# Softmax attention in two passes: the first pass runs three units ahead of its consumer instead of two, TensorE's block work moves in front of its second-pass pieces, and VectorE's splits are spread one per step

## What is computed

```
def adaptive_temperature_softmax(logits):
    original_probs = softmax(logits)
    entropy = sum(-original_probs * log(original_probs + 1e-09))
    poly_result = POLY[0]*e2*e2 + POLY[1]*e2*entropy + POLY[2]*e2 + POLY[3]*entropy + POLY[4]
    beta = where(entropy > 0.5, maximum(poly_result, 1.0), 1.0)
    return softmax(logits * beta)
sim = einsum('bhid,bhjd->bhij', q, k) / sqrt(hd), masked above the diagonal
out = einsum('bhij,bhjd->bhid', adaptive_temperature_softmax(sim), v) @ Wo.T + bo
```

## Time and profile before

| | |
|---|---|
| median of three runs | 2244.86 us |
| the profiled execution, its own time | 2242.96 us |
| its span in the trace | 2241.2 us |
| busy in the span | PE 1608.5, DVE 1480.7, ACT 1393.1, POOL 141.7 us |
| attention, from the first exp1 to the end of its last window | 755.4 to 1960 us |
| ACT busy in the attention's windows | 1051.0 of 1204.6 us |

### The profile page before, as it was taken

How to read it: one execution, slowest core, us unless ns; L and a number is a source line. 1 busy time by engine, 2 the same in 40 slices (tenths; PEclk the granted TensorE clock), 3 DMA queues, 4 the chain that set the end, 5 groups by cost and what they waited for, 6 DMA issues and landing times. The chain is left out here.

```text
span 2241.2 us, 22322 instructions
## 1 busy us (share of the span) xinstructions
PE 1608.5 (72%) x6402; PEld 689.7 (31%) x6402; DVE 1480.7 (66%) x3478; ACT 1393.1 (62%) x2635; POOL 141.7 (6%) x126
## 2 busy tenths in 40 slices
PE   4787899999999643777767778667777787511166
PEld 2443344444444201222222222223222233201144
DVE  6645354535464798887787787877878774479922
ACT  3564443434333697899987999879999997300012
POOL 0000000000000100000000000000000000035365
PEclk9898899999999755676666765666666769755578
DMA  4000065454556201101011010010110103240031
GB/s 146 0 0 0 13 162 156 131 154 132 155 150 171 58 32 39 62 33 62 24 39 60 33 50 34 31 71 26 42 40 28 54 13 98 58 122 0 0 102 49
DMA packets 56667, 147.36 MB, mean 66 GB/s; under 512 B 7760, under 2 KB 22480, under 8 KB 53936
## 3 DMA queue, kind: packets, MB, share of 16 engines
q1 hardware_dynamic: 52320, 136.63, 20.6%
q0 software_dynamic: 3072, 8.39, 1.2%
q10 hardware_dynamic: 1152, 0.92, 0.3%
HBM read 126.38 MB, written 19.53 MB: 65 GB/s over the span
## 5 line engine op out<-in xcount | busy, mean ns | idle before, releaser
L1682 DVE CUSTOM_DVE_ANT_0 sa_lg<-sa_e,sa_lg 128x1024 f32<-128x1024 f32 (+7 forms) x512 | 386.4, 755 | 93.4 <-ACT sa_lg L1573 92.9
L1423 PE MATMUL sa_ps<-sa_space 72*128 72x512 bf16 (+3 forms) x768 | 293.0, 450 | 212.5 <-DVE sa_nmax L1673 148.0
L1563 ACT ACTIVATE sa_e<-sa_e,sa_nmax 128x1024 f32<-128x1024 f32 (+7 forms) x512 | 415.9, 812 | 36.2 <-DVE sa_nmax L1673 36.1
L1673 DVE CUSTOM_DVE_ANT_0 sa_e<-sa_ps,sa_mask 128x1024 f32<-128x1024 f32 (+7 forms) x512 | 385.5, 753 | 71.3 <-PE sa_ps L1423 69.9
L1573 ACT ACTIVATE sa_lg<-sa_e,sa_sum 128x1024 f32<-128x1024 f32 (+7 forms) x512 | 414.9, 810 | 5.1 <-DVE sa_prod L1682 4.6
L1581 ACT ACTIVATE sa_p<-sa_ps 128x512 f32<-128x512 f32 x576 | 345.8, 626 | 40.8 <-PE sa_ps L1475 30.9
L1472 PE MATMUL sa_ps<-sa_q2s,sa_k2s 75*128 75x512 bf16 (+3 forms) x768 | 298.0, 432 | 66.9 <-ACT sa_p L1581 55.2
L974 DVE TENSOR_TENSOR mx_hw<-mx_spread,mx_h 128x512 f32<-128x512 f32 x256 | 176.0, 691 | 232.8 <-PE mx_ps L813 193.3
L875 ACT ACTIVATE mx_h<-mx_ps 128x512 f32<-128x512 f32 (+1 forms) x264 | 157.0, 597 | 277.0 <-PE mx_ps L800 256.4
L800 PE MATMUL mx_ps<-mx_f,m 128*128 128x512 f32 x512 | 262.0, 597 | 0.8 <-ACT mx_h L875 0.8
L813 PE MATMUL mx_ps<-mx_hw,m 128*128 128x512 f32 x512 | 259.9, 594 | 0.6 <-DVE mx_hw L974 0.6
(11 more groups left out here) (322 smaller groups left out, 1864.3 us busy)
## 6 DMA issues: line engine op xcount, KB each, us to landing
mx_spread<-mx_spill SPq DMA_DIRECT2D x256, 256.0 KB, 4.0
sa_space<-sa_spill_q SPq DMA_DIRECT2D x96, 96.0 KB
sa_space<-sa_spill_k SPq DMA_DIRECT2D x96, 96.0 KB
sa_k2s<-sa_spill_k SPq DMA_DIRECT2D x48, 192.0 KB
sa_q2s<-sa_spill_q SPq DMA_DIRECT2D x48, 192.0 KB
m<-m_in SPq DMA_DIRECT2D x1, 4256.0 KB, 18.7
records<-sa_e SPq DMA_DIRECT2D x8, 512.0 KB, 5.2
be_w<-w_in SPq DMA_DIRECT2D x16, 256.0 KB, 12.5
```

The source lines that it names most:

```text
L1423: last = nc.tensor.matmul(out[:, col:col + w], q_ring[:, c % 2, local, i * P:(i + 1) * P], k_ring[:, c % 2, local, col:col + w], start=Tru ...
L1563: nc.scalar.activation(e[:, u % 5, 0:w], e[:, u % 5, 0:w], ACT.Exp, scale=-1.0, bias=nmax[:, b % 2, i, h:h + 1], accum_out=sums[:, b % 2, ...
L1673: nc.vector.tensor_tensor_reduce(out=e[:, u % 5, 0:w], in0=slot_of("unit", u)[:, 0:w], in1=mask_wide[:, SEQ - w:SEQ], scale=1.0, scalar=3. ...
L1682: nc.vector.tensor_tensor_reduce(out=lg[:, u % 2, 0:w], in0=e[:, u % 5, 0:w], in1=lg[:, u % 2, 0:w], scale=1.0, scalar=0.0, op0=ALU.mult, ...
```

## The change

- `AHEAD` goes from 2 to 3: score and evacuate of unit u + 3 are issued at step u. The prologue does three units instead of two.
- On TensorE the loop over `pieces2_at(u + 1)` moves from behind the score to the end of the step, behind all blocks.
- The block steps move so that TensorE still finds the unit ahead in the other slot: `WIDE_AT` 7 to 8, `SHIFT_AT` 9 to 10, `A_AT` 83 to 84, `Q_AT` 87 to 86, `K_AT` 89 to 94, `V_AT` 107 to 108, and `TURN_AT`, `ATT_AT`, `PROJ_AT` each one later.
- VectorE's chains are dealt out: `temper` at step 3, `set_beta` at 4, `split_shift` at 5; the splits of the widened queries at 9, 10, 11 (two) and 12; those of the projected queries at 87, 88, 90, 91 and 92; those of the keys at 95, 97 and 99.
- Three second-pass banks, five `e` buffers, two `lg` buffers and every instruction's shape stay. The number of instructions stays. SyncE's program is the same row by row.

```diff
-AHEAD = 2
+AHEAD = 3
...
-        WIDE_AT, SHIFT_AT = 7, 9
-        A_AT, Q_AT, K_AT, V_AT = 83, 87, 89, 107
-        TURN_AT, ATT_AT, PROJ_AT = 9, 13, 17
+        WIDE_AT, SHIFT_AT = 8, 10
+        A_AT, Q_AT, K_AT, V_AT = 84, 86, 94, 108
+        TURN_AT, ATT_AT, PROJ_AT = 10, 14, 18
...
-            yield from (("unit", 0), ("unit", 1))
+            yield from (("unit", u) for u in range(AHEAD))
...
                     if u + AHEAD < ALL1:
                         score(u + AHEAD)
-                    for m in pieces2_at(u + 1):
-                        second(m)
-                        if m % GROUP == GROUP - 1 and m >= GROUP:
-                            answer(m // GROUP - 1)
                     if (k := side_at(u, WIDE_AT)) is not None:
                         widen(k)
...
                     if (b := scores_at(u, 18)) is not None:
                         score_experts(b)
+                    for m in pieces2_at(u + 1):
+                        second(m)
+                        if m % GROUP == GROUP - 1 and m >= GROUP:
+                            answer(m // GROUP - 1)
...
                     if (k := side_at(u, 2)) is not None:
                         entropy(k)
+                    if (k := side_at(u, 3)) is not None:
                         temper()
-                    if (k := side_at(u, 3)) is not None:
+                    if (k := side_at(u, 4)) is not None:
                         set_beta(k)
-                    if (k := side_at(u, 4)) is not None:
+                    if (k := side_at(u, 5)) is not None:
                         split_shift(k)
...
-                    for r in (8, 9, 10):
-                        if (k := side_at(u, r)) is not None:
-                            split_q2(k, range(2 * (r - 8), min(5, 2 * (r - 8) + 2)))
+                    for r, steps in ((1, range(0, 1)), (2, range(1, 2)), (3, range(2, 4)), (4, range(4, 5))):
+                        if (k := side_at(u, WIDE_AT + r)) is not None:
+                            split_q2(k, steps)
...
                     if (b := batch_at(u, Q_AT)) is not None:
                         take_q(b)
-                        split_q(b, range(0, 3))
-                    if (b := batch_at(u, Q_AT + 1)) is not None:
-                        split_q(b, range(3, 5))
+                    for r, step in ((1, 0), (2, 1), (4, 2), (5, 3), (6, 4)):
+                        if (b := batch_at(u, Q_AT + r)) is not None:
+                            split_q(b, (step,))
                     if (b := batch_at(u, K_AT)) is not None:
                         take_k(b)
-                    if (b := batch_at(u, K_AT + 1)) is not None:
-                        split_k(range(2, 4))
-                    if (b := batch_at(u, K_AT + 2)) is not None:
-                        split_k(range(4, 5))
+                    for r, step in ((1, 2), (3, 3), (5, 4)):
+                        if (b := batch_at(u, K_AT + r)) is not None:
+                            split_k((step,))
```

8 lines of the change are left out of this document (4 added, 4 removed).

## The result

The changed kernel takes 2260.02 us (median of 12 runs) against 2245.07 us for the kernel before (12 runs, same chip): 1.0062 times as long, with a 95% interval of 1.0052 to 1.0072. It is 0.6% **slower** where the prediction said about 0.9% faster. The profiled execution took 2260.62 us with a span of 2258.7 us, against 2241.2 before.

A forecast was written before the change was run, and what follows sets the result against it. It took ACT as the attention's full engine, idle only around blocks, where DVE is nearly the bound. 6.0 + 0.8 + 13.0 + 0 = 19.8 us off 2242.96 gave 2223.2; plus 1.9 for the median, 2225 us, range 2206 to 2246.

The forecast's parts named there:

- A new wait: Away from blocks on DVE, evacuate(u + 3) directly behind the product it waits for: 0.12 us each, bounds 0 and 0.23.
- 154 waits: New waits in stretches where DVE is the bound: about 154, 18.5 us, of which 4.0 fall into idle time.
- First stretch, side 0 and first projections: DVE becomes the bound and is 3.4 us late at side 0; better spread then pays for the wait: 0.
- Sides' ends: Shift earlier, fewer evacuation waits: 1.5 us less in four windows (6.0), 0.4 in two with layernorm behind (0.8).
- Projections: Two windows like 1160 to 1244: splits no longer bunched, 84 us becomes 77.5, 6.5 us less each, 13.0 in all.
- Tail: Steps beyond the first pass's units: DVE runs free, the chain over HBM starts from the same splits: 0.
- Those of the order: Projection windows' ACT idle 18.5 to about 12 us, evacuation waits well below 36, `take_shift` about 2 to 3 instead of 3.7.
- Those of the wait: First stretch: product to evacuation 0.12 us more, first exp1 to that of unit 64 about 3 us more.
- Rival 2: Slower: new wait and late products, in the first stretch and windows after blocks, eat everything; 2251 us, chance 0.12.
- turning point of 0.25 us: Size of the new wait at which the gain of 20 us over about 154 waits turns into a loss.
- Rival 1: DVE is not the bound and the wait is free, all blocks hidden: about 2200 to 2210 us, chance 0.2.
- Rival 3: Order swap and later steps cancel, waits only change their names: 2 to 4 us less, 2242 us, chance 0.1.

The follow-up runs named there:

- E2: The kernel before with four of its five e buffers used, so evacuate(u + 2) waits for its direct predecessor product(u - 2): 2253.92 us, 1.0096 of the kernel before.
- E1: The changed kernel with six e buffers instead of five, so evacuate(u + 3) waits for product(u - 3): 2224.94 us, 0.9974 of the kernel before.
- E3: The changed kernel with five e buffers and, from step 512 on, pieces in front of the blocks again: 2242.75 us, 1.0049 of the kernel before.
- E4: The changed kernel with six e buffers and, from step 512 on, pieces in front of the blocks again: 2221.45 us, 0.9958 of the kernel before.
- E12: The kernel before with only TensorE's pieces moved behind the blocks, still two units ahead: 2229.04 us, 0.9995 of the kernel before.
- E15: The kernel before with AHEAD 3, blocks one step later, six e and three lg buffers, pieces in front, chains bunched: 2213.18 us, 0.9933 of the kernel before.
- E5: The changed kernel with six e buffers, three lg buffers and pieces in front from step 512 on: 2230.39 us, 0.9934 of the kernel before.
- E7: The kernel before with AHEAD 3, blocks one step later, six e and two lg buffers, pieces in front, chains bunched: 2237.2 us, 0.9959 of the kernel before.

## Why the prediction was wrong

**The step that failed** is "A new wait": "I take 0.12 us", between bounds of 0 and 0.23. It measured 0.22, and 0.23 in E2. The reasoning was that "the 0.11 of the plain pair covers a tail of that size", the accumulator read's 0.08. It doesn't: 0.08 and 0.11 add up, and 0.03 more. (The bound of 0.23 was to be these two in full, but they make 0.19; the measured wait lies above their sum.) The Trainium skill, "VectorE: DVE Perf Modes", section "The DRAIN you can't avoid", would have 0 for a semaphore between chained instructions; the 0.11 us of the earlier trace rows and the 0.22 here are against it. The linked pair comes 62 times in the first stretch, where DVE had 4.0 us of idle time. E1 against the changed kernel puts the wait at 0.9% of the time, about 20 us; the traces have 10.3 of it in the first stretch and 18.8 by exp1(511). (For the same pair E3 and E4 the traces have 27.1 by exp1(511), so what lies outside the first stretch is known to some 8 us only.)

The wait decides the sign, as E1 shows, but the prediction's own sum would not have said so. With 0.22 in place of 0.12 its 154 waits cost 15.4 us more, which makes 2240, still a little faster than 2245. The rest is what the prediction put at nothing: the piece behind `widen` at the sides, and the tail.

*First stretch, side 0 and first projections: predicted 0 (3.4 late, won back).* It came out at +12.0, 11.1 late and nothing won back. With 0.22 the prediction's own formula gives 62 x 0.22 - 4.0 = 9.6 for the first part. Without the wait (E1, E4) 0.8 of the 11.1 remain, and the whole is at +0.5.

*Sides' ends: predicted 6.0 + 0.8 us less.* They came out at 4.7 more. In the three sides' windows together ACT's idle time went from 36.3 to 40.2 us. Waits for evacuations fell from 9.4 to 0 and `take_shift` from 21.5 to 12.2, but waits for pieces (L1472) rose from 0 to 14.0, for products from 0.5 to 6.1 and for layernorm's subtraction (L96) from 4.6 to 7.5. Over the whole attention `take_shift` fell by 29.0 - 17.6 = 11.4 over eight, more than the 1.0 each that was taken. What the prediction left out is that the piece behind `widen` waits for the block (2.35 us on ACT in the timeline). That alone doesn't carry the loss, since E12 has the same piece order and loses nothing at the sides (12.1 us for pieces, but 13.3 less in `take_shift`); nor do the dealt-out chains alone, since E15 lacks them and loses 4.3. Which part of the change brings the rest stays open.

*Projections: predicted 13.0 us less.* 9.7 less, and 15.5 with six buffers (E4). The size was about right once the wait is gone, though some 4 us of it are uncertain (E3 against the changed kernel, above). Bunched chains three ahead do as well: E15 has 12.7 less and E5, with dealt-out chains, 12.8; E7 has 17.7 in an execution 6.3 us below its median. So here it is the depth that wins and not the spread, which the prediction didn't tell apart.

*Tail: predicted 0.* 5.9 more. "Nothing hidden there comes out" looked at DVE, the chain over HBM and SyncE, and not at PE, where the pieces moved behind the last layernorm's blocks. E3, E4 and E12 show it from both sides.

*Last units, 480 to 511: not in the sum.* 3.3 more; E12 has 2.6 of it.

So 19.8 us less became 17.5 more in the profiled execution (15.0 in the medians), a difference of 37.3: 12.0 from the start, 11.5 from the sides, 3.3 each from the projections and the last units, 5.9 from the tail, and 1.3 outside these.

**The signs.** Those of the order came: ACT's idle time in the window of the second projections fell from 18.5 to 14.0 us (12 was forecast), its waits for evacuations to 2.4, and `take_shift` waits 2.2 us on average. Those of the wait did not: 0.22 us instead of 0.12, and 11.1 us more to the exp1 of unit 64 instead of 3.

**The rivals.** Rival 2 is the one that came nearest: slower, by the new wait, decided where DVE has no room. Its sign is there: log1 waits 34.3 us for products (over 30), 8.4 of them in the first stretch. Its other half is not: it let the projections' 13.0 vanish through late products, and 9.7 of it stayed, with 11.3 us of log1's waits there. Its price of 6 us was less than half of the 15 measured, and its turning point of 0.25 us too high, since the sides and the tail had no gain to spend. The prediction gave it a chance of 0.12. Rival 1 supposed the wait free. Without the wait the order does win (E1, E4), but 0.3 to 0.4%, where the rival had 1.5 to 2. Rival 3 has a share: with the wait gone, much of what a third logarithm buffer removes comes back under another name.

**What stays open.** Three ahead alone, dealt-out chains alone, and all together with the pieces behind stop at the same 0.4% with two logarithm buffers; the first and the last stop at 0.7% with three (dealt-out chains alone weren't run with three). That a block's work has to pass ACT, PE and DVE in turn whatever their order would explain it, but that was only argued; a run with shorter blocks wasn't made. The sides' term has no cause shown, and nor has the 0.3 to 0.4% that dealing out the chains costs with pieces in front.

## What to carry to other kernels

When a pipeline is made one step deeper, count the buffers again: a ring that was slack by two instructions can become a wait on the instruction directly in front, and that costs at every step, where the engine has least room, and not only at the blocks that the depth was meant for. Where such a cost lies between two bounds and the sign hangs on it, price the verdict at the upper bound before choosing (here about 2242 us, no gain worth the name). And moving a block ahead of steady work on an in-order queue has to be priced for who waits for the steady work, in the tail too, where the reason for moving it is gone.

## What the runs showed of the hardware

A VectorE instruction that waits on a semaphore of its direct predecessor starts 0.11 us later than an unlinked one when both are plain, but 0.22 to 0.23 us later when the predecessor writes an accumulator (the changed kernel, E2). Unlinked, the next instruction overlaps the accumulator read completely (E1). TensorE's granted clock was 0.80 in the tail of the changed kernel and 0.83 before, a mean between its two levels of 1.2 and 2.4 GHz, and its 612 matmuls there took 90.1 us instead of 87.3; with the order of the tail undone (E4) they took 86.8 at 0.83. The lower clock isn't what makes the tail long: E1's tail, with the pieces still behind, took 129.1 us at 0.83. What lowered the clock in the changed kernel's tail isn't shown.
